# Project-stage arithmetic all on VectorE, norm scalings on ScalarE, and the scan's first matrix laid over the normalised rows

## The reference

```
x   = x + mamba(layernorm(x));   x = x + ffn(layernorm(x))

mamba(x): xn = normalised x * ln_w + ln_b            # a second normalisation of the same rows
          xi, z = split(xn @ W_in)                   # 512 channels each
          u = silu(causal_conv4(xi) + conv_b)
          dt_r, B, C = split(u @ W_xproj)            # 16, 64, 64
          delta = softplus(dt_r @ W_dt + b_dt)
          h_t = h_(t-1) * exp(delta_t * A) + (delta_t * u_t) * B_t      # 512 x 64 states
          y_t = h_t . C_t;   out = x + ((y + u * D) * silu(z)) @ W_out
```

## Time and profile before

| | us |
|---|---|
| median of 3 runs | 6069.9 (6068.98 to 6071.72) |
| the profiled execution, its time | 6068.98 |
| the profiled execution, its span | 6067.2 |
| DVE busy in the span | 5520.7 (91%) |
| PE busy, mean granted clock | 5249.1 (87%), 0.975 |
| ACT busy | 3368.2 (56%) |
| POOL busy | 2596.0 (43%) |

### The profile page before, as it was taken

How to read it: one execution, slowest core, us unless ns; L and a number is a source line. 1 busy time by engine, 2 the same in 40 slices (tenths; PEclk the granted TensorE clock), 3 DMA queues, 4 the chain that set the end, 5 groups by cost and what they waited for, 6 DMA issues and landing times. The chain is left out here.

```text
span 6067.2 us, 147986 instructions
## 1 busy us (share of the span) xinstructions
PE 5249.1 (87%) x37915; PEld 2525.2 (42%) x38396; DVE 5520.7 (91%) x3491; ACT 3368.2 (56%) x7982; POOL 2596.0 (43%) x6848
## 2 busy tenths in 40 slices
PE   2898848888888998888988888988888988879998
PEld 1333323444444444444444444444444444436665
DVE  8799968999999999999999999999999999964433
ACT  1676645666666666666666666666666666631111
POOL 4244454444444444444444444444444444420000
PEclk9988869999999999999999999999999999989999
DMA  4788872222222222222222222222222222233232
GB/s 147 277 295 300 292 262 58 53 54 53 53 55 52 54 55 52 54 55 52 55 55 52 54 54 53 55 53 53 55 52 54 55 52 54 55 100 108 95 106 66
DMA packets 1105505, 547.14 MB, mean 90 GB/s; under 512 B 753744, under 2 KB 1015056, under 8 KB 1105056
## 3 DMA queue, kind: packets, MB, share of 16 engines
q1 hardware_dynamic: 1093776, 533.89, 32.6%
q10 hardware_dynamic: 11664, 12.52, 0.6%
HBM read 296.83 MB, written 249.82 MB: 90 GB/s over the span
## 5 line engine op out<-in xcount | busy, mean ns | idle before, releaser
L971 DVE TENSOR_TENSOR_SCAN s_h<-s_decay,s_ubank 128x1024 f32<-128x1024 f32 x2048 | 4460.8, 2297 | 34.5 <-ACT s_ubank L936 33.0
L923 ACT ACTIVATE s_decay<-s_abank 128x512 f32<-128x512 f32 x4096 | 2210.4, 595 | 2.1 <-PE s_abank L861 1.1
L846 PE MATMUL s_ybank<-s_h,s_window 128*8 128x256 f32 x16416 | 1947.9, 602 | 1.9 <-DVE s_h L971 1.9
L887 PE MATMUL s_ubank<-s_x,s_w 128*128 128x256 bf16 x8192 | 1245.8, 275 | 453.2 <-DVE s_h L971 375.6
L1008 POOL TENSOR_TENSOR s_carry<-s_decay,s_h 128x64 f32<-128x64 f32 x2032 | 881.1, 434 | 1750.4 <-ACT s_decay L923 1575.2
L936 ACT ACTIVATE s_ubank<-s_seed 128x64 f32<-128x64 f32 x2048 | 478.2, 233 | 1709.0 <-PE s_ubank L887 1344.5
L861 PE MATMUL s_abank<-s_x,s_a 128*128 128x256 bf16 x8192 | 1254.5, 274 | 53.6 <-DMA s_w<-scratch_b_rows 50.7
L887 PEld LDWEIGHTS s_ubank<-s_x,s_w 128*128 128x128 bf16 x8192 | 675.7, 98 | 1198.0 <-DVE s_h L971 1098.3
L861 PEld LDWEIGHTS s_abank<-s_x,s_a 128*128 128x128 bf16 x8192 | 758.4, 98 | 215.8 <-issue 51.0
L1012 POOL TENSOR_TENSOR s_seed<-s_carry,s_first 128x64 f32<-128x64 f32 x2048 | 657.9, 321 | 164.5 <-ACT s_first L929 4.1
L846 PEld LDWEIGHTS s_ybank<-s_h,s_window 128*8 128x8 f32 x16416 | 377.0, 97 | 839.3 <-issue 730.3
(11 more groups left out here) (123 smaller groups left out, 3196.9 us busy)
## 6 DMA issues: line engine op xcount, KB each, us to landing
s_x<-scratch_u_rows SPq DMA_DIRECT2D x4096, 32.0 KB
scratch_u_rows<-p_u_turn SPq DMA_DIRECT2D x90, 1024.0 KB, 6.4
scratch_delta_rows<-p_dparts SPq DMA_DIRECT2D x136, 512.0 KB, 5.7
s_x<-scratch_delta_rows SPq DMA_DIRECT2D x1024, 64.0 KB, 2.7
scratch_y<-s_y SPq DMA_DIRECT2D x1036, 16.0 KB
scratch_sz<-p_sz SPq DMA_DIRECT2D x16, 1024.0 KB, 5.8
scratch_u<-p_u SPq DMA_DIRECT2D x16, 1024.0 KB, 7.3
s_w<-scratch_b_rows SPq DMA_DIRECT2D x256, 64.0 KB, 2.4
```

Source lines behind the costliest of these rows:

```text
L846: last = nc.tensor.matmul(y_bank[32 * ct:32 * ct + WIN, 1 - x, :], window[:, of, (at + t) * WIN:(at + t + 1) * WIN], H[:, 1 - x, :, t], st ...
L887: last = nc.tensor.matmul(dst.rearrange("p q (a t) -> p a q t", t=2), w2[:, g, 4 * s + 2 * x + e, :], x2[:, s, :, 2 * x + e, q:q + 32, :], ...
L923: nc.scalar.activation(dst.rearrange("p x q t -> p q x t"), a_bank[:, b].rearrange("p j r (x t) -> p (j r) x t", x=2), ACT.Exp).then_inc(e ...
L971: nc.vector.tensor_tensor_scan(H[:, x, PT * p:PT * p + PT, :].rearrange("p q t -> p (q t)"), decay[:, x * (1 + c % 2), p].rearrange("p q t ...
```

## The change

Four edits.

1. The project stage's arithmetic on GpSimd moves to VectorE: `du` goes behind `softplus`, each third part behind its second in `split`, and the four b operations stand together behind both (`split_b`). GpSimd has no loop left in this stage.
2. In the norm stage VectorE no longer scales the rows. It makes `shift` = -mean * rstd (128x4), and ACT makes rstd * x + shift, four activations a tile and normalisation. ACT's loop becomes one over pairs: the scalings to `xa`, those to `xn`, then both tiles' way out of PSUM.
3. `x1` gets no memory of its own but is a bf16 view of `xnT`, which now lives on through the scan stage. VectorE clears all of `xnT` at the end of the project stage, once PE has read the last rows, and GpSimd no longer does it in the scan stage.
4. The scan stage's one semaphore `cleared` becomes three, each waited for where it is needed; the window is cleared first, `x2` in two halves, and H by GpSimd.

```diff
@@ -192,11 +194,10 @@
 ...
                 nc.vector.tensor_scalar(veps[:, s, k, :], mv[:, s, k, :, 1], EPS, None, ALU.add).then_inc(veps_done, 1)
-            def scaled(j, s, k, src, dst, done):
+            def shifts(j, s, k):
                 dve.wait_ge(rstd_done, j * 4 + k * 2 + s + 1)
-                for g in range(SUB):
-                    nc.vector.tensor_scalar(dst[:, g, :], src[:, g, :], mv[:, s, k, g, 0:1],
-                                            rstd[:, s, k, g:g + 1], ALU.subtract, ALU.mult).then_inc(done, 1)
+                nc.vector.scalar_tensor_tensor(out=shift[:, s, k, :], in0=mv[:, s, k, :, 0], scalar=-1.0,
+                                               in1=rstd[:, s, k, :], op0=ALU.mult, op1=ALU.mult).then_inc(shift_done, 1)
             count = [0]
@@ -223,14 +224,12 @@
 ...
                 for s in range(2):
-                    dve.wait_ge(res_done, j * 2 + s + 1)
-                    scaled(j, s, 0, x[:, 2 * r + s], xa[:, 2 * r + s], xa_done)
+                    shifts(j, s, 0)
                 for s in range(2):
 ...
                 for s in range(2):
-                    dve.wait_ge(tr_done, j * 2 + s + 1)
-                    scaled(j, s, 1, xa[:, 2 * r + s], xn[:, s], xn_done)
+                    shifts(j, s, 1)
             over_pairs(dve, pair)
@@ -302,14 +301,31 @@
 ...
             act.wait_ge(par_loaded, 32)
-            with act.Fori(0, NT // 2) as j:
+            def scaled(j, s, k, src, dst, done):
+                act.wait_ge(shift_done, j * 4 + k * 2 + s + 1)
+                for g in range(SUB):
+                    nc.scalar.activation(dst[:, g, :], src[:, g, :], ACT.Identity, bias=shift[:, s, k, g:g + 1],
+                                         scale=rstd[:, s, k, g:g + 1]).then_inc(done, 1)
+
+            def turned_out(j, s):
+                act.wait_ge(tr_done, j * 2 + s + 3)
+                for k in range(KD):
+                    nc.scalar.activation(xnT[:, k, bass.ds((j * 2 + s) * TW, TW)], tr[:, s, k, :], ACT.Identity,
+                                         bias=lnb[:, k:k + 1], scale=lnw[:, k:k + 1]).then_inc(tr_read, 1)
+                act.wait_ge(res_done, j * 2 + s + 5)
+                act.dma_start(rv[j * 2 + s], res[:, s]).then_inc(res_stored[s], 16)
+
+            def pair(j, r):
                 for s in range(2):
-                    act.wait_ge(tr_done, j * 2 + s + 3)
-                    for k in range(KD):
-                        nc.scalar.activation(xnT[:, k, bass.ds((j * 2 + s) * TW, TW)], tr[:, s, k, :], ACT.Identity,
-                                             bias=lnb[:, k:k + 1], scale=lnw[:, k:k + 1]).then_inc(tr_read, 1)
-                    act.wait_ge(res_done, j * 2 + s + 5)
-                    act.dma_start(rv[j * 2 + s], res[:, s]).then_inc(res_stored[s], 16)
+                    act.wait_ge(res_done, j * 2 + s + 1)
+                    scaled(j, s, 0, x[:, 2 * r + s], xa[:, 2 * r + s], xa_done)
+                for s in range(2):
+                    act.wait_ge(tr_done, j * 2 + s + 1)
+                    scaled(j, s, 1, xa[:, 2 * r + s], xn[:, s], xn_done)
+                for s in range(2):
+                    turned_out(j, s)
+
+            over_pairs(act, pair)
             for s in range(2):
@@ -657,12 +673,15 @@
 ...
                                                op0=ALU.max, op1=ALU.add).then_inc(delta_done, 1)
+                dve.wait_ge(u3_done, i + 2)
+                dve.wait_ge(delta_done, i + 2)
+                nc.vector.tensor_tensor(du[:, :, :], lw[:, :, :], u[:, c % 2], ALU.mult).then_inc(du_done, 1)
             def split(i):
-                for src, rest, parts, free, first, whole, one, left, two in (
+                for src, rest, parts, free, first, whole, one, left, two, three, had in (
                         (lw, w1, dparts, (dparts_stored, i * (16 * NCB) + 16 * NCB), delta_done, i + 2, d1_done, dr_done,
-                         d2_done),
-                        (du, du, uparts, (turned, i * 8 + 16), du_done, i + 3, u1_done, ur_done, u2_done)):
+                         d2_done, d3_done, 1),
+                        (du, du, uparts, (turned, i * 8 + 16), du_done, i + 3, u1_done, ur_done, u2_done, u3_done, 2)):
                     dve.wait_ge(first, whole)
@@ -670,23 +689,34 @@
 ...
                     nc.vector.tensor_copy(parts[:, 1], rest[:, :, :]).then_inc(two, 1)
-
-            def step(i, c, b, ahead1, ahead2):
-
-                softplus(i)
-                if ahead2:
-                    front(*ahead2)
+                    dve.wait_ge(two, i + 1)
+                    nc.vector.tensor_tensor(parts[:, 2], rest[:, :, :], parts[:, 1], ALU.subtract).then_inc(three, 1)
+
+            def split_b(i):
                 dve.wait_ge(back_read, i * 7 + 13)
 ...
                 nc.vector.tensor_copy(b_parts[:, 0], b_in[:, :]).then_inc(b1_done, 1)
-                split(i)
+                dve.wait_ge(b1_done, i + 1)
+                nc.vector.tensor_tensor(b_rest[:, :], b_in[:, :], b_parts[:, 0], ALU.subtract).then_inc(br_done, 1)
                 dve.wait_ge(br_done, i + 2)
                 nc.vector.tensor_copy(b_parts[:, 1], b_rest[:, :]).then_inc(b2_done, 1)
+                dve.wait_ge(b2_done, i + 1)
+                nc.vector.tensor_tensor(b_parts[:, 2], b_rest[:, :], b_parts[:, 1], ALU.subtract).then_inc(b3_done, 1)
+
+            def step(i, c, b, ahead1, ahead2):
+
+                softplus(i, c)
+                if ahead2:
+                    front(*ahead2)
+                split(i)
+                split_b(i)
             front(0, 0, 0)
 ...
             over_tiles(dve, step)
+            dve.wait_ge(in_ready, NT * 8)
+            nc.vector.memset(xnT[:, :, :], 0.0)
         @block.gpsimd
@@ -699,25 +729,9 @@
 ...
                                     pattern=[[-1, P]], channel_multiplier=1).then_inc(ident_ready, 1)
-            pool.wait_ge(cleared, 2)
-
-            def step(i, c, b, ahead1, ahead2):
-                pool.wait_ge(u3_done, i + 2)
-                pool.wait_ge(delta_done, i + 2)
-                nc.gpsimd.tensor_tensor(du[:, :, :], lw[:, :, :], u[:, c % 2], ALU.mult).then_inc(du_done, 1)
-                pool.wait_ge(b1_done, i + 1)
-                nc.gpsimd.tensor_tensor(b_rest[:, :], b_in[:, :], b_parts[:, 0], ALU.subtract).then_inc(br_done, 1)
-                pool.wait_ge(d2_done, i + 1)
-                nc.gpsimd.tensor_tensor(dparts[:, 2], w1[:, :, :], dparts[:, 1], ALU.subtract).then_inc(d3_done, 1)
-                pool.wait_ge(u2_done, i + 1)
-                nc.gpsimd.tensor_tensor(uparts[:, 2], du[:, :, :], uparts[:, 1], ALU.subtract).then_inc(u3_done, 1)
-                pool.wait_ge(b2_done, i + 1)
-                nc.gpsimd.tensor_tensor(b_parts[:, 2], b_rest[:, :], b_parts[:, 1], ALU.subtract).then_inc(b3_done, 1)
-
-            over_tiles(pool, step)
-
-
-def scan_stage(nc, d):
+
+
+def scan_stage(nc, d, xnT):
     with ExitStack() as ctx:
@@ -732,7 +746,8 @@
 ...
         none = sb("s_none", [P, PT])
-        x1 = sb("s_x1", [P, 2, ROWS, HALVES, SLOTS, 2 * T], BF16)
+        x1 = xnT[:, :, :].rearrange("p k t -> p (k t)").bitcast(BF16)
+        x1 = x1.rearrange("p (g r f j t) -> p g r f j t", g=2, r=ROWS, f=HALVES, j=SLOTS)
         x2 = sb("s_x2", [P, 2, 4, 4, PAIRS, 2], BF16)
@@ -781,7 +796,6 @@
 ...
             sp.dma_start(a_w[:, :, :, :].rearrange("p f j m -> p (f j m)"), d["a_image"]).then_inc(a_loaded, 16)
-            sp.wait_ge(cleared, 5)
             deltas = d["delta_rows"].rearrange("c (h f j r) t -> r (c h) f j t", h=2, f=HALVES, r=ROWS)
@@ -792,6 +806,7 @@
 ...
             def store_y(f, s, taken):
+                sp.wait_ge(y_cleared, 1)
                 sp.wait_ge(y_read, taken)
@@ -809,9 +824,11 @@
 ...
                 if c % 2 == 0:
+                    sp.wait_ge(w2_cleared, 1)
                     for h in range(2):
 ...
                                      bs[:, bass.ds(f * 4 + 2 * TW // 8, 8), :]).then_inc(rows_loaded[g], 16)
+                sp.wait_ge(x2_cleared, c % 2 + 1)
                 for r in range(8):
@@ -954,12 +971,12 @@
 ...
         def _(dve):
-            nc.vector.memset(yout[:, :, :, :], 0.0).then_inc(cleared, 1)
+            nc.vector.memset(window[:, :, :], 0.0).then_inc(window_ready, 6)
+            nc.vector.memset(yout[:, :, :, :], 0.0).then_inc(y_cleared, 1)
             nc.vector.memset(y_bank[:, :, :], 0.0).then_inc(y_read, 2)
-            nc.vector.memset(w2[:, :, :, :], 0.0).then_inc(cleared, 1)
-            nc.vector.memset(x2[:, :, :, :, :, :], 0.0).then_inc(cleared, 1)
-            nc.vector.memset(window[:, :, :], 0.0).then_inc(window_ready, 6)
-            nc.vector.memset(H[:, 1], 0.0).then_inc(scan_done, 8)
+            nc.vector.memset(w2[:, :, :, :], 0.0).then_inc(w2_cleared, 1)
+            for s in range(2):
+                nc.vector.memset(x2[:, s], 0.0).then_inc(x2_cleared, 1)
             def chunk(it, f, c):
@@ -978,8 +995,7 @@
 ...
         def _(pool):
```

(11 more changed lines are left out.)

## The result

The changed kernel takes 5962.54 us (median of 6 runs, 5960.74 to 5964.18) against 6069.44 (6 runs, 6068.19 to 6071.72): a ratio of 0.9824, 95% interval 0.9811 to 0.9836. It is faster by 107 us; 5958 had been forecast, in a range of 5938 to 5986. The profiled execution took 5963.24 us with a span of 5961.4, against 6068.98 and 6067.2 before.

The account below looks back on a forecast made before the run. VectorE's instruction stream was taken to set the project and scan stages' length. Savings of 7.5 + 67.9 + 5.2 + 4.4 + 26.9 = 111.9 us from 6068.98 gave 5957.1, with the median 0.9 above: 5958 us, range 5938 to 5986.

Parts of the forecast that it names:

- VectorE's hold by GpSimd: Project stage: each VectorE instruction beside a GpSimd operation seems to do its whole work after GpSimd lets go.
- 13.8 us taken away: Project step: VectorE's stalls beside GpSimd, on w1, its follower, `du`, `lw` and conv multiplications, go away.
- 8.6 added: Project step: 8.0 us for operations moved to VectorE, and 0.6 for five dependent starts.
- fourteen steps: Project stage: a step goes from 41.7 to 36.5 us, over fourteen steps -67.9 us.
- second-last step: Project stage, first of two steps without conv: from 32.1 to 26.9 us, -5.2.
- The next bound: Project step, rival: PE, ACT or the stores bound it; PE's 37.8 us a step gives 5976 us; chance 0.15.
- 0.8 us of cover: Project step: the ACT and PE side needs 35.7 us even if nothing in it gets faster, against VectorE's 36.5.
- ScalarE's wait for w1: Project step: ACT's idle time before w1 falls from 5.98 us to about 1 to 2.
- The last stretch: Project stage's end, set by queued stores: 53.7 us where it was 58, -4.4.
- the head: Scan stage's start: SP's first load no longer waits for GpSimd's two clearings of 13.75 us; -26.9, or -24 if late.
- The clearing's end: Project stage's last stretch: clearing `xnT` takes 13.9 us, ends at 40.8, under the stores' 53.7, costing nothing.
- The norm ring: Norm stage: a pair of tiles becomes a ring through three engines, 14.6 us instead of 15.93; -7.5 in all.

Follow-up runs that it names:

- without the loop: The kernel after with the project stage's three loop rounds written out and nothing else: 5958.00 us.
- the kernel that clears twice: The kernel after with VectorE's clearing of the normalised rows (`xnT`) done twice: 5969.17 us.
- `du` back: The kernel after with one moved operation, `du` (128x2048), put back on GpSimd, all else staying on VectorE: 5985.50 us.
- additions: The kernel after with GpSimd adding two tensors (128x512) into a tile nobody reads, four times each project step: 6014.69 us.
- shown alone: The kernel before with the last two edits alone (scan's first matrix laid over the normalised rows, cleared by VectorE at the project stage's end): 6042.28 us.
- The looser one: The kernel after with residual additions moved from GpSimd to VectorE and ScalarE turning out the previous pair between its two groups of scalings: 5957.86 us.

## Why the forecast came out right, and where not

- **VectorE's hold by GpSimd** carried the forecast, and is shown: disjoint data stretch VectorE by 0.95 us an addition of 512 columns, and one operation put back costs 4.26. The 13.8 us taken away and 8.6 added gave 36.5 a step; it is 36.63, or 36.60 without the loop.
- **The fourteen steps** are the term that was mis-sized, by 4.8 of 67.9 us. 1.8 is the 0.13 a step; 3.0 is the three longer steps. In the first, no table load stands ahead of the `xi` that VectorE waits 0.85 us for; PE begins that tile's products 3.35 us after w1 in this execution (205.59), and 2.56 in that of the kernel that clears twice, whose first step is 36.79. What made PE later is open. The other two come with ScalarE's jump back. ScalarE's table load at the loop's top was in the trace before, at 338.15, and cost nothing in a step of 41.7; the forecast asked what else waits in the middle of a round and not at its top. It isn't the load alone, which is there at every top. In the kernels with steps of 38.50 (`du` back) and 40.43 (additions) the fourth and eighth step are no longer than the rest. And in the kernel that clears twice, whose project loop is the same code, they are 37.68 and 36.63, so this part comes and goes from one execution to the next. PE's timeline in its eighth step, and then the busy times around it, for 465 to 470 us, in that kernel and in the kernel after:

```profile
465.68 1.99 PE L495 MATMUL p_in<-xnT,p_w_in 128*128 x4 [1.85 <-ACT p_xi L568]
```

```profile
465.00:470.00 5.00, 4.32 (x21) 2.22 (x22) 4.86 (x3) 4.42 (x8) 0.00 (x0) 1.00 0.17 66
```

```profile
465.00:470.00 5.00, 3.27 (x7) 1.29 (x8) 4.86 (x3) 3.98 (x5) 0.00 (x0) 0.73 0.20 67
```

  Behind a wait of 1.85 us PE's group took 1.99 at a granted clock of 1.00; behind one of 2.93 it took 3.25, with the clock at 1.2 GHz for a part of these five microseconds. So `xi` is late where the clock falls after PE's longer idle time, which the load starts; that the clock alone decides is argued from these tops, not shown by a run. PE waited a microsecond less at the one because it came later: its products with `W_dt` and `W_xproj` ahead of it had taken 4.40 and 9.96 us there, and 3.88 and 8.83 in the kernel after. The second of each pair, in PE's timeline there and then in the kernel after:

```profile
449.49 9.96 PE L502 MATMUL p_bk<-p_u,p_w_x 128*128 128x512 f32 x16
```

```profile
450.00 8.83 PE L501 MATMUL p_bk<-p_u,p_w_x 128*128 128x512 f32 x16
```

  The mean granted clock over PE's 23 us ahead of the top was 0.85 there and 0.93 in the kernel after; why it differed stays open.
- **The next bound**: I left 0.8 us of cover under the step; it is 2.2. PE's mean granted clock went from 0.87 before to 0.92, from the first to the last w1, and its wait of 3.89 us a step for GpSimd's last part has become 0.4 at most, for VectorE's; it is busy 513.08 us of these 542.
- **ScalarE's wait for w1** was forecast to fall to 1 to 2 us. It fell to 2.6 to 4.6 in most steps, because exp comes sooner than I had it, and to 1.5 and 0.8 in the two behind the tops.
- **The last stretch, the head, the second-last step** came out within 0.1 us each, and the head is shown alone (-27.3). The clearing's end was forecast at 40.8 after the last w1 and came at 44.0, since the 3.4 us ahead of it were not counted; the 9.5 us of cover that were left hid this.
- **The norm ring**: the period 14.6 is 14.45, and eight scalings take 4.04, estimated at 3.9. The looser one, with 12.1, bears out that a ring of waits set the period. That the whole term is right to 0.1 us is partly luck: from the first pair's second pow (31.27, forecast at 31.0) to the last's (132.70) the pairs gave 0.8 us more than forecast, and the start and the end 0.9 less.
- From the first scan to the end the kernel after takes 1.3 us more. None of it lies in the scans, which take 4462.4 us from the first's start to the last's end, against 4462.7; the output stage takes 1.6 us more, 1.0 of it ahead of VectorE's first operation there, which waits 18.23 us for a load instead of 17.19. The cause is open.

## What to carry to other kernels

Where VectorE sets the pace, count what GpSimd does beside it as VectorE's own time: if the same operation costs VectorE less than GpSimd's hold, move it over, and look for the sign first, pairs of durations that end a fixed time after GpSimd's. Ask of each thing that cost nothing before, a table load or a jump back, what hid it, above all at a loop's first step. And when an edit far away changes a loop's time, look at where the loop's code stands in its engine's stream: the same loop cost 5.2 us a jump at one place and nothing at another.

## What the hardware showed that I had not expected

- The hold works in turns, both ways: GpSimd's addition of 512 columns was recorded at 3.2 us beside a busy VectorE, of which 2.2 was its wait for it. GpSimd's recorded durations are so no measure of its own work.
- A copy of 512 columns by GpSimd costs VectorE 0.29 us, an addition 0.95.
- A clearing of 16384 words takes 17.2 us, of which the record shows 13.71 behind 3.36 to 3.48 of "issue"; one of 4096 has 3.47 behind 0.80, and in the kernel before one of 8192 has 6.88 behind 1.66. The gap grows with the memset, so it belongs to it.
- ScalarE's jump back stalls for 5.23 us, with instruction packets in the trace, when its loop of 268 instructions begins at the 190th instead of the 138th.
